# Preparing the second expert layer inside the attention before it: groups of two batches, in pieces, in a loop written out

## The reference: what is computed

```python
x = x + attn_a(layernorm(x), ...)   # 16 heads of 8, sparse mask
x = x + ffn(layernorm(x), ...)      # 8 experts, one per token
x = x + attn_b(layernorm(x), ...)   # 16 heads of 64, causal
x = x + ffn(layernorm(x), ...)      # the same experts again

# ffn:
aff = x @ centroids.T
assign = jnp.argmax(aff, axis=1)
order = jnp.argsort(assign)
xs, es = x[order], assign[order]
alpha = sigmoid(take(aff[order], es))
h  = relu(layernorm(xs, ln_g[e], ln_b[e]) @ w1[e].T + b1[e])   # 128 -> 512
ye = xs + h @ w2[e].T + b2[e]                                  # 512 -> 128
out = (alpha * y + (1 - alpha) * xs) back in the old order
```

## Time and profile before

| | us |
|---|---|
| runs (3) | 586.84, 582.73, 582.52 |
| median | 582.73 |
| profiled execution, its own time | 583.51 |
| its span | 581.7 |
| attention b, from its first full step to the last output projection | 212 to 482 |
| preparation of FFN 2 up to its first slot on PE | 482 to 524 |
| slots of FFN 2 on PE | 524 to 572 |

### The profile page before, as it was taken

One profiled execution on the slowest core, in us unless ns is written; L12 is line 12 of the kernel. 1 busy time (PEld: TensorE's weight loads), 2 busy tenths in 40 slices (PEclk: granted clock), 3 DMA queues, 4 the chain that ended last, 5 costly groups with the idle time before them and its releaser, 6 DMA issues.

```text
span 581.7 us, 10958 instructions
## 1 busy us (share of the span) xinstructions
PE 466.7 (80%) x3500; PEld 367.0 (63%) x3500; DVE 370.0 (64%) x1090; ACT 229.2 (39%) x835; POOL 235.5 (40%) x245
## 2 busy tenths in 40 slices
PE   3957994608986299999999999999999964509993
PEld 2323663508985167787878778787877754409893
DVE  6599877734574477757675775667577527635672
ACT  2710003303442056636554663655466333304441
POOL 5003883562444234434243443424344324552443
PEclk9979997557999599999999999999999977558997
DMA  9999400126462200000000000000000000126560
GB/s 319 402 422 420 204 1 1 49 99 183 120 193 74 64 0 2 1 2 1 0 0 0 0 0 0 0 0 0 0 0 1 0 2 1 63 98 183 140 201 23
DMA packets 21861, 47.50 MB, mean 82 GB/s; under 512 B 3233, under 2 KB 13480, under 8 KB 19394
## 3 DMA queue, kind: packets, MB, share of 16 engines
q1 hardware_dynamic: 18818, 40.73, 20.3%
q0 software_dynamic: 3008, 6.34, 3.1%
HBM read 23.82 MB, written 24.15 MB: 82 GB/s over the span
## 4 chain that ended last, share of the span: by engine, by line
issue 79%; PE 15%; SPq 2%; DMA 2%; ACT 0%; POOLq 0%; POOL 0%; DVE 0%; ACTq 0%
PE ps L820 7%; PE ps L833 7%; PE ps L810 1%; DMA pv<-sorted_in 1%; DMA pv<-in_w 0%; DMA after_ffn<-pv,dest 0%; SPq L409 0%; SPq L357 0%; POOLq L142 0%; SPq L373 0%; SPq L370 0%; ACT pv L584 0%; DVE pv L1260 0%; SPq L376 0%; ACT pv L594 0%
## 5 line engine op out<-in xcount | busy, mean ns | idle before, releaser
L493 POOL TENSOR_TENSOR vT<-vT,prec 128x256 f32<-128x256 f32 (+1 forms) x128 | 103.2, 826 | 168.0 <-DVE prec L1321 168.0
L616 ACT ACTIVATE vT<-ps,nmax 128x128 f32<-128x128 f32 (+1 forms) x256 | 105.1, 434 | 26.0 <-DVE nmax L1313 26.0
L624 ACT COPY prod<-ps 128x384 f32<-128x384 f32 x96 | 42.9, 481 | 117.6 <-PE ps L920 114.2
L1313 DVE TENSOR_REDUCE nmax<-ps 128x2 f32<-128x256 f32 (+1 forms) x128 | 62.4, 550 | 33.9 <-PE ps L900 33.9
L865 PE MATMUL ps<-xnT,wb 128*128 128x256 f32 x256 | 67.0, 385 | 4.6 <-DVE xnT L1293 3.9
L920 PEld LDWEIGHTS ps<-cst,vT 128*128 128x128 f32 x384 | 44.7, 141 | 18.7 <-issue 15.8
L616 ACT ACTIVATION_READ_ACCUMULATOR vT<-ps,nmax 128x1 f32 x256 | 56.1, 219 | 0.0
L920 PE MATMUL ps<-cst,vT 128*128 128x128 f32 x384 | 52.5, 273 | 1.8 <-POOL vT L493 1.7
L933 PE MATMUL ps<-prod 128*64 128x256 f32 (+1 forms) x512 | 49.8, 337 | 3.1 <-ACT prod L624 2.1
L833 PE MATMUL ps<-w2s,pv 128*128 (+1 forms) x368 | 50.0, 279 | 2.0 <-issue 2.0
L894 PE MATMUL ps<-qk 64*128 64x128 f32 (+1 forms) x512 | 51.0, 338 | 0.0
(11 more groups left out here) (151 smaller groups left out, 829.9 us busy)
## 6 DMA issues: line engine op xcount, KB each, us to landing
sorted_in<-zero SPq DMA_DIRECT2D x1, 16512.0 KB, 58.5
pv<-in_w SPq DMA_DIRECT2D x30, 259.0 KB
pv<-sorted_in SPq DMA_DIRECT2D x46, 129.0 KB
wps<-in_w SPq DMA_DIRECT2D x1, 2072.0 KB, 9.2
w2s<-in_w SPq DMA_DIRECT2D x1, 2048.0 KB, 13.2
wb<-in_w_b SPq DMA_DIRECT2D x1, 1536.0 KB, 17.5
xres<-in_x SPq DMA_DIRECT2D x4, 256.0 KB, 3.8
xres<-after_ffn SPq DMA_DIRECT2D x4, 256.0 KB, 3.8
```

The source lines that it names most:

```text
L493: last = nc.gpsimd.tensor_tensor(px, px, view(prec, m_at(n, x) + t * 2, [[1, 2], [0, (t + 1) * P]]), ALU.mult)
L616: last = nc.scalar.activation(pb[:, o:o + (t + 1) * P], wide[:, c:c + (t + 1) * P], ACT.Exp, bias=nmax[:, m:m + 1], accum_out=psum[:, m:m ...
L624: nc.scalar.copy(pT[:, c:c + BLOCKS * P], bank[hh][:, 0:BLOCKS * P]).then_inc(b_pa, 1)
L1313: last = nc.vector.tensor_reduce(nmax[:, m:m + 2], view(wide, x * 1024 + t * P, [[512, 2], [1, (t + 1) * P]]), AX.X, ALU.max, negate=True)
```

## The change: what it does

The groups of FFN 2 become two whole batches each: `place_of` maps tile p of group order to the tile of `xres`. Group h (0, 1, 2) can then be prepared as soon as attention b has added batch 2h+1, which is in the first step of batch 2h+2. Its preparation is cut in pieces that stand at the end of the eight steps that follow; `group_at` gives group h and step d within it. The fourth group is prepared after attention b as before. In group h:

- d = 0, 1: DVE means, then spread. d = 2: POOL powers, DVE norm.
- d = 3: PE `turn_v` (into bank 1 now), ACT copy and residual.
- d = 4: PE `affinity`, DVE choose. d = 5: DVE count, ACT exp.
- d = 6: PE `rank`, DVE place. d = 7 and d = 0, 1, 2 of the next group: POOL one indirect DMA each.

POOL's part of step 32 doesn't exist, so the four DMAs of group 2 come behind its last division. Means and variances of the FFNs have a tile `fmv` of their own. The steps of attention b are no loop any more but 32 steps in a row on each engine. FFN 1 is as it was. PE has new waits in the pieces, and before transposes that overwrite a bank.

```diff
-        def all_steps(eng, step, lead, tail):
-
-            for i in range(-lead, STEPS):
+        def all_steps(step, lead, tail):
+
+            for i in range(-lead, NB * STEPS + tail):
                 step(*at(0, i))
-            with eng.Fori(1, NB - 1) as b:
-                for j in range(STEPS):
-                    step(b, j)
-            for i in range(STEPS + tail):
-                step(*at(NB - 1, i))
+
+        def group_at(n):
+            return divmod(nth(n) - 2 * STEPS - 1, 2 * STEPS)
+
+        def place_of(k, p):
+            return p if k == 0 else p % GT // 2 * NB + p // GT * 2 + p % 2
...
+            def step(b, j):
+                n = (b, j)
+                divide(b, j)
+                h, d = group_at(n)
+                if 0 <= h < NG - 1 and d == 2:
+                    powers(1, h)
+                if 0 <= h < NG - 1 and d == 7:
+                    dispatch(1, h, [0])
+                if 1 <= h and d < GT - 1:
+                    dispatch(1, h - 1, [d + 1])
...
+            all_steps(step, 0, 0)
+            dispatch(1, NG - 2)
+            powers(1, NG - 1)
+            dispatch(1, NG - 1)
...
+                h, d = group_at(n)
+                if 0 <= h < NG - 1 and d == 3:
+                    turned_v(1, h)
+                    residual(1, h)
+                if 0 <= h < NG - 1 and d == 5:
+                    exps(1, h)
...
@@ turn_p
                         need(pe, b_pa, 3 * nth(n))
+                        h, d = group_at(n)
+                        if 0 <= h < NG - 1 and d == 4:
+                            pe.wait_ge(f_vTs, NG + h + 1)
...
                         need(pe, b_pd, nth(n))
+                        h, d = group_at(n)
+                        if 0 <= h < NG - 1 and d == 5:
+                            pe.wait_ge(f_oh, NG + h + 1)
+                        if 0 <= h < NG - 1 and d == 7:
+                            pe.wait_ge(f_row, NG + h + 1)
...
@@ PE's step, between project_qk(n2, 1) and turn_xb, out_proj_b, values_b
+                h, d = group_at(n)
+                if 0 <= h < NG - 1 and d == 3:
+                    pe.wait_ge(b_pa, 3 * nth(n) + 3)
+                    turn_v(1, h)
+                if 0 <= h < NG - 1 and d == 4:
+                    pe.wait_ge(b_pd, nth(n) + 1)
+                    affinity(1, h)
+                if 0 <= h < NG - 1 and d == 6:
+                    pe.wait_ge(b_pd, nth(n) + 1)
+                    rank(1, h)
...
@@ the end of DVE's step
+                h, d = group_at(n)
+                if 0 <= h < NG - 1:
+                    if d == 0:
+                        dve.wait_ge(b_x, 2 * h + 2)
+                        means(1, h)
+                    if d == 1:
+                        spread(h)
+                    if d == 2:
+                        norm(1, h)
+                    if d == 4:
+                        choose(1, h)
+                    if d == 5:
+                        count(1, h)
+                    if d == 6:
+                        place(1, h)
...
+            all_steps(step, 3, 1)
+            dve.wait_ge(b_x, NB)
+            means(1, NG - 1)
+            spread(NG - 1)
+            norm(1, NG - 1)
+            choose(1, NG - 1)
+            count(1, NG - 1)
+            place(1, NG - 1)
+            tables(1)
             ffn(1)
```

More of the change, by code:

```diff
@@ L456, in dispatch @@
                 pool.wait_ge(f_al, n)
-                for t in range(g * GT, (g + 1) * GT):
+                for i in tiles:
+                    t = g * GT + i
                     nc.gpsimd.indirect_dma_start(
@@ L606, in ffn @@
                         normed(s + 2)
+            for g in range(NG + 1):
+                if g < NG:
+                    residual(0, g)
+                    turned_v(0, g)
+                if g > 0:
+                    exps(0, g - 1)
+            act.wait_ge(in_f, 4 * 16)
             ffn(0)
@@ new lines, in turn_v, with affinity @@
+            def turn_v(k, g):
+                pe.wait_ge(f_vh, k * NG + g + 1)
+                need(pe, f_vTs, k * NG + g)
+                for i in range(GT):
+                    t = g * GT + i
+                    last = nc.tensor.transpose(bank[k][:, i * P:(i + 1) * P], pack[:, t * ROW:t * ROW + D], ident)
+                last.then_inc(f_vT, 1)
+            def affinity(k, g):
+                pe.wait_ge(f_vTs, k * NG + g + 1)
+                for i in range(GT):
+                    c = aff_at[k][g] + i * NE
+                    last = nc.tensor.matmul(wide[:, c:c + NE], vTt[:, i * P:(i + 1) * P], cent_s[:], start=True, stop=True)
+                last.then_inc(f_aff, 1)
@@ L806, in turn_x, with totals @@
+            def totals(k):
+                pe.wait_ge(f_hs, (k + 1) * NG)
+                for h in range(NG):
+                    last = nc.tensor.matmul(wide[:, total_at:total_at + NE], ones_bf[:],
+                                            hsum[:, h * NE:(h + 1) * NE], start=h == 0, stop=h == NG - 1)
+                last.then_inc(f_total, 1)
+            def ffn(k):
                 def turn_x(s):
@@ L848, in ffn @@
                 output(NSLOT - 1)
+            pe.wait_ge(a_x, NU)
+            pe.wait_ge(in_r, 1)
+            pe.wait_ge(in_f, 4 * 16)
+            for g in range(NG + 1):
+                if g < NG:
+                    turn_v(0, g)
+                    affinity(0, g)
+                if g > 0:
+                    rank(0, g - 1)
+            totals(0)
             ffn(0)
@@ L965, in _ @@
             pe.wait_ge(b_w, 1)
-            all_steps(pe, step, 3, 1)
+            all_steps(step, 3, 1)
+            turn_v(1, NG - 1)
+            affinity(1, NG - 1)
+            rank(1, NG - 1)
+            totals(1)
             ffn(1)
@@ L1271, in ffn @@
                 finish(NSLOT - 1)
+            dve.wait_ge(a_x, NU)
+            nc.vector.tensor_copy(view(pack, 2 * D + 1, [[ROW, NT]]), cst[:, C_TOKEN:C_TOKEN + NT])
+            for g in range(2):
+                means(0, g)
+                spread(g)
+            for g in range(NG + 2):
+                if g < NG:
+                    norm(0, g)
+                if g + 2 < NG:
+                    means(0, g + 2)
+                    spread(g + 2)
+                if 0 <= g - 1 < NG:
+                    choose(0, g - 1)
+                    count(0, g - 1)
+                if 0 <= g - 2:
+                    place(0, g - 2)
+            tables(0)
             ffn(0)
```

372 lines of the change are left out of this document (164 added, 208 removed).

## The result

| | us |
|---|---|
| kernel before, median of 4 runs (range) | 582.92 (582.52 to 586.84) |
| kernel after, median of 4 runs (range) | 565.08 (562.08 to 566.51) |
| ratio, 95% interval | 0.9661 [0.9611, 0.9711] |
| profiled execution after, its own time and its span | 566.51 and 564.7 |
| forecast | 568.0, range 564.0 to 576.0 |

On the 582.73 us of before that the forecast was made against, the ratio gives 563.0 us, interval 560.1 to 565.9. That is 5.0 us under the forecast and 1.0 us under the low end of the range. Both lie inside the range, near its low end; over the three, the forecast is 1 to 5 us too high. Part of that is in the terms of the sum, and part in something that the range had no room for.

The account below looks back on a forecast made before the run. PE bounds attention b (236.18 of 237.10 us busy); POOL's send queue ends FFN 2's preparation. From 583.51: -18.6 + 5.2 - 1.8 + 0.5 = -14.7, 568.8, less 0.8 for the median: 568.0 us; range 564 to 576.

Parts of the forecast that it names:

- Tail: Between attention b and FFN 2's first slot: one group's chain and four sends remain; -18.6 us, bounds -15.1 and -19.8.
- rank's result stays late: Rival, last group's place in FFN 2: rank's result still 4.7 us late, total 571.5 to 573.5 us; chance 0.20.
- PE in attention b: Three groups' transposes, affinity and counting matmuls on a full PE: 1.74 us each at full clock, +5.2 us together.
- my low bound: PE's added work in attention b: at least 4.2 us, for the affinity's and most of the transposes' loads.
- Stalls: Attention b: pieces moved onto DVE, ACT and POOL plus PE's new waits, priced at +0.5 us; bound some 9 us.
- DVE's 1.83 us of idle time: Each attention b step: DVE idles 0.78 us before copying values' output, 1.05 before the maxima; every piece fits, maxima on time.
- the cases at 572.5 to 577: Rival, attention b gets stalls: 572.5 us at half of the 9 us bound, 577 at the bound; chance 0.15.
- the 3.1 us of that rival: Rival, POOL's sends in attention b starved by DVE: costs 1 to 3 us, 570; skill's send figure 3.1 us; chance 0.04.
- Loop: Attention b written out: plain PE steps 7.40 instead of 7.55 us, two in each of six batches; -1.8 us, bounds 0 and -1.8.
- Group 2's sends: After attention b's last division: four sends need 5.1 us of POOL, start around 475, have some 9 us before last power.
- Slower than before: Rival, DVE and POOL become attention b's bound: pieces paid at full length, 603 us if all are; chance 0.03.
- slots at full clock: Rival, FFN 2: PE's slots begin at full clock because the hole before them is shorter; 566 us, chance 0.03.

Follow-up runs that it names:

- the sixteen sends above: Changed kernel, but groups 2 and 3 prepared together after attention b and all sixteen sends issued behind their two powers; 574.75 us (1 run).
- the kernel with late sends: Changed kernel, but the twelve sends of groups 0 to 2 issued after attention b, behind the last group's power; 572.27 us, ratio 0.9823.
- the doubled `means`: Changed kernel with `means` issued twice in its step for groups 0 to 2; 571.56 us in one run.
- two with filling: Changed kernel plus unread matmuls on PE: behind attention b only, 567.7 us; also in attention b's last steps, 563.96 us.
- two with two groups: Changed kernel, but groups 2 and 3 prepared after attention b: eight sends behind, 574.84 us; those sends held until the last place, 574.62 us.
- the filling in both places: Changed kernel plus unread matmuls on PE behind attention b and in attention b's last three steps; 563.96 us, ratio 0.9674.

## Why the forecast was some 3 us too high, step by step

**Tail, forecast -19.8 + 1.2.** The chain was right to 0.2 us: it gives 21.9 us from the residual to the first slot without a late rank, and 21.76, 21.82 and 21.77 were measured. The step that failed is the 1.2 us for *rank's result stays late*: 0 was measured. I had written that the 4.7 us of FFN 2 might belong to the sends under way, and then priced the place where none are under way by FFN 1, where sends are under way too (before: from 108 us on, place at 115.39). Lateness appears only in stretches with sends under way: FFN 2 of the kernel before, the one with the loop written out (2.98 us), the sixteen sends above, the tables of the kernel with late sends, and FFN 1, where DVE's idle time before the last place varies from 0 to 2 us among executions of the same code. Without sends under way it was under 0.1 us in all eight profiles (three of the changed kernel, the doubled `means`, two with filling, two with two groups). So that rival didn't merely fail to happen; the condition under which it was seen is gone. Sends alone don't suffice, though: `place` was on time in the kernel with late sends.

Why PE's signal comes late is open. The Trainium skill ("SBUF — State Buffer", who interferes with whom) lets GpSimd and DVE block each other when DVE runs in a mode that takes both ports, or reads two inputs from SBUF while GpSimd reads SBUF. The first instruction of `place` reads one input from PSUM and one from SBUF, so by that rule it has nothing to wait for, and the trace agrees: DVE started 0.02 to 0.03 us after each recorded signal. Another cause isn't excluded: the recording itself. In the first profile of the changed kernel only 7 of the semaphores' rises are missing, and there FFN 1, sixteen sends and all, has no lateness; in the other eleven profiles 99 to 154 are missing, nearly all in FFN 1 and FFN 2, where indirect DMAs are issued, and in each of them FFN 1's place or tables are late. Whether an execution that isn't profiled has this lateness, no run here tells.

**PE in attention b, forecast +5.2, measured +4.2.** The step that failed is the size of each piece. I halved the durations of isolated groups of matmuls at half clock, and such a duration runs from the first start to the last end. In a full queue the next matmuls start before that end (after the `turn_v` of 316.78, which lasts 0.60, the output projection starts at 317.22), and a piece costs only the spacing that it adds: `affinity` has a row of 1.00 us in attention b and adds 0.90, `turn_v` a row of 0.60 and adds 0.32, `rank` adds 0.20. That is 1.42 of the 1.74 priced. The value at my low bound was the right one, and the bubbles at the switches that I gave the high bound for weren't there.

**Stalls, forecast +0.5, measured 0.** Every step of a kind has the same length in all groups, within 0.04 us, and steps without a piece on PE didn't grow. The argument by DVE's 1.83 us of idle time held, with two corrections. The idle time before the maxima did vanish behind `norm`. And the doubled `means` shows how near the edge is, so the cases at 572.5 to 577 had their place. Sends in attention b weren't starved: the eight in its steps took 1.01 to 1.06 us each, nothing like the 3.1 us of that rival.

**Loop, forecast -1.8, measured -1.77 in the steps**, and not seen in the kernel's time. The longer program loads more code, 29 and 23 packets against 18 and 17 over the whole kernel, and no step is longer for it. This is what the Trainium skill ("Runtime: NRT & Kernel Launch", instruction fetch) leads one to expect of straight code, and the trace agrees. That the two packets of the earlier trace rows were PE's code, as I wrote, the row doesn't say: the profile names queues there, not engines. What the 0.15 us of a step in the loop was, no run here tells.

**Group 2's sends.** The outcome was right and the margin wrong: I had them start around 475 with some 9 us to spare. They waited 3.81 us for place, started at 480.56, and left 3.5.

**Slower than before, and slots at full clock.** Neither came. From slot to end the changed kernel takes 56.7 to 58.4 us against 58.0. The price of the second was wrong as well: the filling in both places brought the slots at full clock, and the stage was no shorter (59.75 us).

**What the sum had no term for.** The terms that failed make 1.2 + 1.0 + 0.5 = 2.7 us, and bring 568.0 to 565.3, beside a median of 565.08. The rest, down to the 563.0 of the first ratio, isn't shown to be the change's: 565.3 lies within the interval, and two repeats give 565.0 and 566.8. I set the low end at my three best terms and took 1 us for everything else. The three stretches other than the steps and the tail vary by more than that. The clearest is the end of attention b in executions of one kernel: 15.83 us where the granted clock stayed at 1.00 up to the last residual, 17.18 where it was 0.50 from 478.3 to 481.7, and 19.76 where it was 0.50 from 474.5 to 484.8. The last output projection of the changed kernel, 32 passes, in its first and second profile:

```profile
482.36 3.84 PE L905 MATMUL ps<-wob,prod 128*128 128x128 f32 x32 [0.79 <-DVE prod L1355]
```

```profile
479.42 6.37 PE L905 MATMUL ps<-wob,prod 128*128 128x128 f32 x32 [0.79 <-DVE prod L1355]
```

A range for a change of this size needs 2 to 3 us on either side for that alone.

## What to carry to other kernels

Work that a full engine must do costs what it adds to the spacing of its neighbours in the queue, not the length of its row when it ran alone; take the spacing from a stretch where the engine is full. When a chain of several groups is cut down to one, cost it as a bare chain, and ask of each delay that was seen before whether its condition is still there. Of the 20 us here, sends that no longer queue up behind the last group make some 7 and the shorter chain the rest, while the price on the full engine is 1.4 us per group as long as each piece on the helping engine fits into that engine's idle time of one step.

## What the runs showed of the hardware

- Where indirect DMAs are issued one behind the other, the semaphore that PE's last matmul raises can be recorded late: 4.66 us after the matmul's end in the kernel before (510.31 against 505.65). DVE waits for it, with the releaser shown as "remote" or "issue". In eight tails without sends under way the wait was under 0.1 us. The cause, the recording included, is open.
- PE's granted clock falls at differing points of identical kernels: 32 passes of the last projection took 3.84 or 6.37 us. With the steps ahead of them, also partly at half clock, that moves the end of attention b by up to 4 us.
- Filling PE's idle time with unread matmuls kept the clock at full through the affinity (1.04 us instead of 1.88). In one profile it fell after the first slot, in the other it stayed at 1.00 to the last one; from the first slot to the end they took 60.94 and 59.75 us, against 58.14 without filling.
- A step of 7.55 us in a hardware loop takes 7.40 when written out, in all 12 places where it shows; ten runs of the whole kernel show no gain (0.9996).
